# A recurrence with a mixture of experts, first quad: TensorE turns keys, values and results; orders of block beginnings, routed beginning and last stores changed

## The reference

```python
def step(carry, kv_t):                      # over the 128 tokens of a sequence
    p, q, o = carry
    kt, vt = kv_t
    no = jnp.maximum(o, u + kt)
    A = jnp.exp(o - no)
    E = jnp.exp(u + kt - no)
    y = (A * p + E * vt) / (A * q + E)
    no2 = jnp.maximum(w + o, kt)
    A2 = jnp.exp(w + o - no2)
    E2 = jnp.exp(kt - no2)
    return ((A2 * p + E2 * vt, A2 * q + E2, no2), y)

# xf = layernorm(x) as rows
gates = softmax(xf @ gate_w + gate_b)                  # 16 experts
topv, topi = top_k(gates, 2)
combine = sum(one_hot(topi, 16) * topv[..., None], axis=1)
h = gelu(einsum('nd,edh->neh', xf, ew1) + eb1)         # h = 128
eo = einsum('neh,ehd->ned', h, ew2) + eb2
routed = einsum('ned,ne->nd', eo, combine)
hs = gelu(einsum('nd,sdh->snh', xf, sw1) + sb1)        # h = 2048, s = 2
shared = einsum('snh,shd->nd', hs, sw2) + sum(sb2)
x = x + wkv(w, u, layernorm(x), ctx)
x = x + shared + routed
```

## Time and profile before

| | |
|---|---|
| median of 3 runs | 903.01 us (898.25 to 903.58) |
| profiled execution | 902.2 us, its span 900.5 us |
| granted TensorE clock over the span | 0.993 |
| busy of the span | TensorE 93%, VectorE 72%, ScalarE 54%, GpSimd 20% |
| memory traffic | 110.58 MB read, 22.98 MB written |

### The profile page before, as it was taken

One profiled execution on the slowest core, in us unless ns is written; L12 is line 12 of the kernel. 1 busy time (PEld: TensorE's weight loads), 2 busy tenths in 40 slices (PEclk: granted clock), 3 DMA queues, 4 the chain that ended last, 5 costly groups with the idle time before them and its releaser, 6 DMA issues.

```text
span 900.5 us, 14811 instructions
## 1 busy us (share of the span) xinstructions
PE 841.0 (93%) x4018; PEld 694.7 (77%) x4018; DVE 646.8 (72%) x1345; ACT 485.7 (54%) x859; POOL 182.6 (20%) x223
## 2 busy tenths in 40 slices
PE   0198999999999999999999999999999999999997
PEld 0066878888788888887888888878888798997885
DVE  6995899855668687655797777555677588883764
ACT  4433776544455656344556564435455378885531
POOL 2001000011200000111100002111122568763660
PEclk9999999999999999999999999999999999999999
DMA  9155334449543333494343334654797368877985
GB/s 224 28 150 151 111 112 132 114 93 186 108 139 107 99 90 83 101 214 106 118 117 94 94 94 91 127 123 140 176 199 200 106 205 244 258 243 275 305 252 162
DMA packets 125855, 134.40 MB, mean 149 GB/s; under 512 B 10256, under 2 KB 87616, under 8 KB 125276
## 3 DMA queue, kind: packets, MB, share of 16 engines
q1 hardware_dynamic: 116844, 108.47, 46.0%
q0 software_dynamic: 8784, 25.11, 9.5%
q10 hardware_dynamic: 160, 0.02, 0.0%
HBM read 110.58 MB, written 22.98 MB: 148 GB/s over the span
## 4 chain that ended last, share of the span: by engine, by line
PE 92%; DVE 3%; DMA 2%; issue 1%; ACT 1%; SPq 1%; POOL 0%; DVEq 0%; POOLq 0%; ACTq 0%
PE up L561 13%; PE up L562 13%; PE up L563 13%; PE acc L623 12%; PE acc L628 12%; PE acc L625 12%; PE up L770 3%; PE up L772 2%; PE acc L561 2%; PE up L684 1%; PE acc L563 1%; PE acc L562 1%; PE misc L588 1%; PE acc L693 1%; PE up L588 1%
## 5 line engine op out<-in xcount | busy, mean ns | idle before, releaser
L561 PE MATMUL up<-xs,w1hi 128*128 128x512 f32 (+1 forms) x512 | 200.0, 391 | 4.6 <-ACT xs L902 4.6
L562 PE MATMUL up<-xs,w1hi 128*128 128x512 f32 (+1 forms) x512 | 196.5, 384 | 0.0
L563 PE MATMUL up<-xs,w1lo 128*128 128x512 f32 (+1 forms) x512 | 196.4, 384 | 0.0
L623 PE MATMUL acc<-w2hi,hhi 128*128 128x512 f32 x490 | 190.9, 390 | 1.3 <-issue 1.3
L625 PE MATMUL acc<-w2lo,hhi 128*128 128x512 f32 x490 | 190.7, 389 | 0.0
L840 ACT ACTIVATE hhi<-up,b_col 128x512 fp32r<-128x512 f32 (+1 forms) x128 | 86.9, 679 | 148.6 <-PE up L563 119.9
L1058 DVE TENSOR_TENSOR hlo<-hf,hhi 128x512 fp32r<-128x512 f32 (+1 forms) x128 | 86.0, 672 | 88.9 <-ACT hf L843 57.5
L628 PE MATMUL acc<-w2hi,hlo 128*128 128x512 f32 x490 | 131.7, 389 | 0.0
L561 PEld LDWEIGHTS up<-xs,w1hi 128*128 128x128 f32 x512 | 96.2, 188 | 23.9 <-ACT xs L902 5.2
L563 PEld LDWEIGHTS up<-xs,w1lo 128*128 128x128 f32 x512 | 96.2, 188 | 19.2
L562 PEld LDWEIGHTS up<-xs,w1hi 128*128 128x128 f32 x512 | 96.3, 188 | 18.3 <-issue 0.2
(11 more groups left out here) (243 smaller groups left out, 1134.0 us busy)
## 6 DMA issues: line engine op xcount, KB each, us to landing
w_raw<-in_L_ffn_sw SPq DMA_DIRECT2D x270, 256.0 KB, 3.1
expert_rows<-ysb SPq DMA_DIRECT2D x47, 256.0 KB, 3.8
vin<-in_ctx SPq DMA_DIRECT2D x16, 256.0 KB, 8.0
xn_rows<-kn POOLq DMA_DIRECT2D x16, 256.0 KB, 8.4
e2raw<-in_L_ffn_ew SPq DMA_DIRECT2D x16, 256.0 KB, 5.1
ew_sb<-in_L_ffn_ew SPq DMA_DIRECT2D x16, 256.0 KB, 7.5
X<-in_x SPq DMA_DIRECT2D x12, 256.0 KB, 10.1
out<-X SPq DMA_DIRECT2D x12, 256.0 KB, 4.4
```

The costliest lines, as they stand in the source:

```text
L561: nc.tensor.matmul(o, lhs[0], rhs[0], start=start, stop=False)
L562: nc.tensor.matmul(o, lhs[0], rhs[1], start=False, stop=False)
L563: return nc.tensor.matmul(o, lhs[1], rhs[0], start=False, stop=stop)
L623: nc.tensor.matmul(acc[t][:], hh, w2hi[:, slot], start=first and (q > 0 or t >= HT) or again, stop=False)
```

## The change

It has five parts. (1) For the first quad TensorE turns keys, values and results by 128x128 transposes (`key_T`, `value_T`, `result_T`); channels lie in another order than in the other quads, so this quad has small tables and vectors of its own (grow0, boost0, a wider wu), and ScalarE takes the exponential and the copies of values straight from PSUM. The recurrence of this quad is written out in a new order on VectorE (`early_es` and the like), with the product for the next half's keys ahead of the addition of results, which comes from PSUM in two parts. The full tables are made on ScalarE later (the decay's one in the first block), three bias copies go from VectorE to ScalarE, the gate weights go behind the second half's statistics. (2) PRE is 5 instead of 7; SP's first loads are cut by halves, two of the first four loads of x are issued by ScalarE, ahead of w and u, and the weight loads go one for one with the products that free their buffers. (3) At a block's end TensorE runs down product c, then `block_ready` and up product c + 2. (4) At the routed beginning GpSimd's second cast and VectorE's second low part go ahead of the wait for the last shared product, and the third weight and row parts ahead of the X additions; `take_rows` comes one step earlier. (5) Of the last 16 stores SP issues eight and ScalarE eight.

```diff
-    PRE = 7
+    PRE = 5
...
-                    sp.wait_ge(wt.sem, wt.at(2 * q - 1, "tv"))
+                    if q == 1:
+                        sp.wait_ge(vT_ps, TB)
+                    else:
+                        sp.wait_ge(wt.sem, wt.at(2 * q - 3, "tv"))
...
+            load_half(0, (0, 1))
+            load_half(1, range(GB))
+            load_values(0)
+            load_values(1)
...
+            for n in range(RING, PRE + RING):
+                if n < PRE:
+                    load_pre_w1(n)
+                else:
+                    sp.wait_ge(pre_up, n - RING + 1)
+                    load_w1(n - PRE, n - PRE, chunk_of(n - PRE))
+                if n < PRE:
+                    load_pre_w2(n)
+                else:
+                    sp.wait_ge(pre_down, n - RING + 1)
+                    load_w2(n - PRE, n - PRE, chunk_of(n - PRE))
...
+                if c >= RING:
+                    load_w2(c, c, chunk_of(c))
...
-                for g in range(GB):
+                for g in (0, 1):
                     sp.dma_start(outq[NQ - 1, g, :, t], X2[32 * g:32 * g + 32, NQ - 1, t]).then_inc(out_done, 16)
...
-                    if isinstance(c, int) and ahead % CH == 0 and ahead < NCH:
-                        block_ready(ahead // CH)
-                    if not isinstance(c, int) or ahead < HOLD or c >= HOLD and ahead < NCH:
+                    new_block = isinstance(c, int) and ahead % CH == 0 and ahead < NCH
+                    more = not isinstance(c, int) or ahead < HOLD or c >= HOLD and ahead < NCH
+                    if more and not new_block:
                         up_product(c + 2, ahead, ahead // CH)
...
                     last.then_inc(down_done, 1)
+                    if new_block:
+                        block_ready(ahead // CH)
+                        up_product(c + 2, ahead, ahead // CH)
...
+                        pe.wait_ge(con.sem, con.at(0))
+                        pe.wait_ge(bias_hi, 3)
...
+            def key_T(tb):
+                pe.wait_ge(kn_ok, tb + 1)
+                bank = up[tb] if tb < HT else acc[tb - HT]
+                for k in range(KC):
+                    last = nc.tensor.transpose(bank[:, P * k:P * k + P], kn[:, tb, P * k:P * k + P], ident[:])
+                last.then_inc(kT_ps, 1)
...
+            def value_T(tb):
+                pe.wait_ge(v_half[tb // HT], 16 * GB)
+                bank = v_bank[tb]
+                for k in range(KC):
+                    last = nc.tensor.transpose(bank[:, P * k:P * k + P], vin[:, tb, P * k:P * k + P], ident[:])
+                last.then_inc(vT_ps, 1)
+
+            def result_T(tb):
+                pe.wait_ge(wkv0.sem, wkv0.at(tb // HT, "y" if tb % HT else "y0"))
+                bank, at = up[tb] if tb < HT else acc[tb], D * (tb % HT)
+                for k in range(KC):
+                    last = nc.tensor.transpose(bank[:, P * k:P * k + P],
+                                               y_cols[:, at + P * k:at + P * k + P], ident[:])
+                last.then_inc(yT_ps, 1)
...
+            for tb in range(HT):
+                key_T(tb)
+            for tb in range(HT):
+                value_T(tb)
...
+            for tb in range(HT, TB):
+                key_T(tb)
+            value_T(HT)
...
+            value_T(HT + 1)
...
+            for tb in range(HT):
+                result_T(tb)
+            pe.wait_ge(v_ok, TB)
...
+            pe.wait_ge(wexp.sem, wexp.at(1, "e"))
+            pe.wait_ge(ek_half, 2)
...
-                if p == PRE - 2:
+                if p == PRE - 1:
                     for tb in range(HT, TB):
                         transpose_x(tb, xn[:, tb], acc[tb])
                 pre_down_product(p)
+                if p == 1:
+                    for tb in range(HT, TB):
+                        result_T(tb)
...
+            def early_exp(tb):
...
+                nc.scalar.activation(ek[:, :, part], bank[:].rearrange("p (c t) -> p c t", t=TT), ACT.Exp,
+                                     bias=shift[:]).then_inc(wexp.sem if tb % HT else ek_half, 1)
...
+            def early_values(tb):
...
+                nc.scalar.copy((vp1 if tb // HT else vp)[:, :, part],
+                               v_bank[tb][:].rearrange("p (c t) -> p c t", t=TT)).then_inc(v_ok, 1)
...
+            def first_tables():
...
+                for b in range(KC):
+                    last = nc.scalar.activation(grow0[:, b], ramp[:], ACT.Exp, scale=w_down[:, CB + b:CB + b + 1])
...
+            def table_boost():
                 for b in range(CB):
-                    act.wait_ge(tab.sem, tab.at(0))
-                    last = nc.scalar.activation(boost[:, b, TH:], ramp[:, TH:], ACT.Relu, bias=cap_uw[:, b:b + 1],
...
+            def table_keep():
+                act.wait_ge(wkv0.sem, wkv0.at(1))
+                nc.scalar.activation(keep[:, :, 1:], w_neg[:, 0:CB].unsqueeze(2).broadcast_to([P, CB, TH]), ACT.Exp)\
...
+            for g in (2, 3):
+                act.dma_start(X2[32 * g:32 * g + 32, 0, 0:HT], xq[0, g, :, 0:HT]).then_inc(x_half[0], 16)
...
-            tables_first()
-            wkv_exp(0)
-            tables_late()
+            first_tables()
+            for tb in range(HT):
+                early_exp(tb)
+            for tb in range(HT):
+                early_values(tb)
+            table_grow()
+            wkv_reciprocal(0)
             act.wait_ge(b1_ps, 1)
             nc.scalar.copy(b1_col[:], misc[:, 0:CH]).then_inc(b1_ok, 1)
-            act.wait_ge(b1_ok, 1)
-            wkv_reciprocal(0)
-            wkv_exp(1)
+            for tb in range(HT, TB):
+                early_exp(tb)
+            for tb in range(HT, TB):
+                early_values(tb)
+            table_boost()
+            act.wait_ge(c_in, 16 * 10)
+            for part in (0, 32, 64):
+                nc.scalar.copy(bias_r[part:part + 32], bias_f[part:part + 32]).then_inc(bias_hi, 1)
             for tb in range(HT):
                 x_full(tb)
             for tb in range(HT):
                 x_hi_again(tb)
-            for p in range(4):
-                pre_gelu(p)
+            pre_gelu(0)
+            pre_gelu(1)
             nc.scalar.preload_act_table_set("natural_log_exp_and_others")
             wkv_reciprocal(1)
+            pre_gelu(2)
+            pre_gelu(3)
+            split_w1(0, 0)
             pre_gelu(4)
-            split_w1(0, 0)
-            pre_gelu(5)
             split_w1(1, 1)
-            pre_gelu(6)
             for tb in range(HT, TB):
                 x_hi(tb, 1, tb, acc[tb])
             split_w1(2, 2)
...
+                        if r == 2:
+                            table_keep()
...
+            for t in range(TB):
+                act.wait_ge(acc_free, TB * (NQ - 1) + len(y_bank) + t + 1)
+                for g in (2, 3):
+                    act.dma_start(outq[NQ - 1, g, :, t], X2[32 * g:32 * g + 32, NQ - 1, t]).then_inc(out_done, 16)
...
+            def early_es(h):
+                after(wexp, h, "e")
+                dve.wait_ge(ek_half, h + 1)
+                after(tabs0, 0, "grow")
+                if h:
+                    after(wkv0, h - 1, "ev")
+                edo(V.tensor_tensor(by_group(es[:, :, 1:]), by_group(ek[:]), early_times(grow0, h), ALU.mult))
...
+            def early_add(h):
+                for tb in range(HT * h, HT * h + HT):
+                    dve.wait_ge(yT_ps, tb + 1)
+                    bank = up[tb] if tb < HT else acc[tb]
+                    V.tensor_tensor(X2[:, 0, tb], X2[:, 0, tb], bank[:], ALU.add).then_inc(x2_ok, 1)
...
             tables()
             early_ln1(0)
+            early_ln1_apply(0)
             early_ln1(1)
-            early_ln1_apply(0)
-            for part in (0, 2, 3, 4, 5):
-                wkv_part(0, 0, part)
+            early_es(0)
+            early_h(0)
+            early_hv(0)
+            early_den(0)
             early_ln1_apply(1)
-            wkv_key_rows(0, 1)
-            wkv_part(0, 0, 7)
-            wkv_part(0, 0, 8)
+            early_num(0)
+            early_result(0)
+            early_es(1)
+            early_add(0)
             early_ln2(0)
-            wkv_value_rows(0, 1)
+            early_h(1)
             early_ln2_apply(0)
-            for part in (2, 3, 4, 5):
...
+            early_hv(1)
+            early_den(1)
+            early_num(1)
+            early_result(1)
             for tb in range(HT):
                 x_lo_again(tb)
-            wkv_part(0, 1, 7)
-            wkv_part(0, 1, 8)
+            early_add(1)
             early_ln2(1)
+            gate_weights()
             split_w1(0, 0)
+            early_ln2_apply(1)
             split_w1(1, 1)
-            early_ln2_apply(1)
             for tb in range(HT, TB):
                 x_lo(tb, 1, tb, acc[tb])
             split_w1(2, 2)
+            bias_low()
...
             routed_x(1)
+            routed_w1(1)
             dve.wait_ge(down_done, HOLD)
-            routed_w1(1)
             routed_sum(0)
```

(7 more changed lines are left out.)

294 lines of the change are left out of this document (179 added, 115 removed).

## The result

The changed kernel takes 888.42 us (median of four runs, 886.83 to 889.47) where the kernel before takes 901.60 (median of four, 898.25 to 903.58): a ratio of 0.985, with a 95% interval of 0.983 to 0.987; the medians are 13.2 apart. The forecast was 887, within 882 to 893.5. The profiled execution took 888.09, its span is 886.5, 14.0 less than before; the sum of the prediction was 15.05 less.

What follows compares the result with a forecast made beforehand. VectorE's beginning was taken to set when TensorE, nearly gapless after 76.75 us, starts the main products. Terms -14.0 + 5.2 - 4.7 + 0 - 1.85 + 0.3 = -15.05 took 902.2 to 887.2; predicted 887, range 882 to 893.5.

Steps and rivals of the forecast that it cites:

- First half, walked through the list: First quad's start on VectorE: first half's rows at 35.9, so TensorE gets them 6.0 us before today's 41.91.
- the wait for the vectors: Start, loads of small vectors now last of six issues on ScalarE: 4.4 us becomes 6.1, layernorm starts at 7.3.
- one product that hides GpSimd's root: End of VectorE's first half: after statistics at 34.1, a product covers GpSimd's root, rows ready at 35.9.
- The second half: Second half of the first quad: rows at 57.6, then a weight load's cast decides; main products at 62.75, 14.0 earlier.
- rival at 890.0: Two ScalarE table loads on the start's path each add a 1.38 us drain, start 2.8 later; 2%.
- Two chunks less ahead: First block: five chunks in plain f32 instead of seven turn two half steps into full ones, +5.2 us.
- Block beginnings: Down product moved ahead of each block's first up product removes three waits and slow first products: -4.7 us.
- the down product is not ready: Block beginnings keep their wait because the down product moved ahead is not ready: 891.9 us; 6%.
- Routed beginning: Second routed product starts 1.1 us earlier, but VectorE's bank-freeing adds come later: 0, between -1.5 and +1.
- Last stores: End of the kernel: half of the 16 stores issued by ScalarE, last issue at 896.5 instead of 898.4: -1.85 us.
- Row additions: Last chunks: first row additions one step earlier, ahead of a step's low parts, may hold TensorE: +0.3 us, at most 1.
- rival at 903.4: TensorE's short bursts keep it at 1.2 GHz through all plain-f32 products, start at 79, slower than before; 4%.

Runs made afterwards that it cites:

- vectors first: Changed kernel with the four loads of vectors w and u ahead of the two loads of x in ScalarE's queue: 890.73 us.
- tokens-first run: Changed kernel with ScalarE's copies and VectorE's low parts of the second half's tokens ahead of the second chunk's weight split: 885.41 us.
- additions first: Changed kernel with VectorE's two bank-freeing additions put back ahead of the third weight and row parts: 888.81 us.
- filled-gap run: Changed kernel with second half's tokens ahead of the weight split and 74 extra identity turns (28 and 46) in TensorE's idle time: 884.88 us.
- 12 and 16 turns: Changed kernel with 28 extra identity turns on TensorE, 12 ahead of the first half's results and 16 behind them: 889.69 us.

## Why the prediction was right, step by step

- **First half, walked through the list.** TensorE has its rows at 37.37, forecast 35.9: 1.5 late, by two steps that failed. One is the wait for the vectors: forecast 6.1 and statistics at 7.3, measured 6.91 and 8.15, in later traces 7.2 to 7.6. The order of six issues was priced, their landing was not. With the vectors first x is next, at 7.7, so neither order reached 7.3. The other is "one product that hides GpSimd's root": the product took 1.23 as forecast, the root 1.60, and VectorE waited 0.58. It takes 1.60 or 1.61 in all nine traces with the changed start and 0.69 at this place in all five with the old one; why was not tested. Between the two steps the list holds within 0.3, and ScalarE's ramps at 128 columns took 6.24, forecast 6.2.
- **The second half.** VectorE's wait of 2 us for the reciprocal (1.86) and what each engine waits for are right, the times about 1.1 late (result by 51.9, measured 53.0). The cast's load as what ends last: right, shown by the tokens-first run. That the start is only 0.7 late, 63.47 against 62.75, is in part luck: of the 1.5 us, 0.4 came back because the first 24 products took 6.91 instead of 7.33, and the load, issued at 57.61 instead of 56.4, landed after 3.13 us, where I had taken 3.9.
- **The table loads** (rival at 890.0, from the Trainium skill, "ScalarE: Activation LUTs", "What ACT_TABLE_LOAD costs"): the logarithm began 0.02 us after the load's row also here. Had a drain come on top, the path would have shown it. No run shows one.
- **Two chunks less ahead.** 5.24 from the earlier trace rows, and 4.8 measured, on the kernel before (175.9 against 171.1) and on the changed one (174.92 against 170.15 with seven). The first block is 5.5 longer than in the run with only the blocks reordered, because the wait at VectorE's scans is 0.75 longer too (1.85 against 1.10), which I had between -1.1 and +1.1. So the block's total is right by errors that cancel. That it costs nothing ahead holds only in the new beginning; both runs with the other number of chunks are slower.
- **Block beginnings.** -4.7; -1.66 at each of the two later ones in the changed kernel, -5.3 for all three alone, a little more than the waits themselves. The rival "the down product is not ready" has nothing.
- **Routed beginning.** 0, bounds -1.5 and +1: +0.5 over the whole routed part in the changed kernel's trace, 7.45 against 7.38 up to the first down product, and -1.0 there when it ran alone, without a gain in its time. The mechanism was right (VectorE's additions hold the fourth tile's turns), and "what follows these is ready then and starts as today" is nearly so: the third up product comes 5.65 us after the first with the old order, 5.35 with the new one at full clock, and 4.45 with the additions moved back. What I left out is the granted clock. It fell at this beginning in all four traces with the old order, in five of the seven with the wait of 2.5 us, and in none of the three with the additions first.
- **Last stores.** -1.85; -1.8. **Row additions:** +0.3; 0.
- **The low clock.** The granted clock was 0.50 in the first 5 us of a stretch I named as a sign of being wrong (38 to 60), and before it: a window of the changed kernel, same columns as above:

```profile
30.00:42.00 12.00, 5.89 (x21) 4.78 (x22) 11.28 (x17) 8.46 (x15) 2.77 (x3) 0.50 0.22 65
```

It was back at 1.00 by 44, and the chunk products ran at 1.88, so the rival at 903.4 stays out. But the slow phase was in my sum without my seeing it as a cost: I had taken 1.94 and 7.33 from the earlier trace rows, where TensorE had idled 27 us. The filled-gap run prices it: its turns and first products took 2.3 us less than the changed kernel's, 3.2 less than with the tokens first alone, and its start came 3.0 earlier than there.

The errors, 0.7 at the start, next to nothing over the three blocks (+0.53 against +0.5), 0.5 in the routed part and 0.05 at the stores, less 0.3 for the row additions, make the 1.0 by which the forecast gain was too large. The sum is nearer than its terms.

## What to carry to other kernels

Walk the new list of the engine that sets the start, instruction by instruction, with durations from the trace, and let every hand-over end with what it waits for: the end of such a walk came out within 0.8 us of 63, though single steps in it were off by 0.4 to 0.9 us both ways: a load's landing and an operation taken as hidden behind another are the ones to give a range. A cast that waits for a load must not stand ahead of work that is ready and is waited for: moving one such split on each of two engines took away a wait of 1.9 us, and with the additions first the median fell by 4.8. How many products to put ahead of a wait is set by the length of the wait; when the wait changes, count again.

## What the runs showed of the hardware that I had not expected

- A granted clock of 1.00 in a window can mean that the trace has no record there. With the tokens first the first 24 plain products took 7.81 us, with the gap filled 5.45; the windows of 38 to 46, same columns, first of tokens first, then of the gap filled, both say 1.00:

```profile
38.00:46.00 8.00, 7.33 (x23) 5.87 (x24) 7.90 (x8) 3.94 (x6) 1.17 (x2) 1.00 0.23 80
```

```profile
38.00:46.00 8.00, 7.29 (x34) 5.70 (x33) 7.90 (x8) 6.65 (x9) 1.04 (x2) 1.00 0.29 98
```

  But the clock records of the tokens-first trace begin only at 45.30, with the upper level (2.4 GHz), and its products start 0.43 us apart up to 45.33 and 0.22 apart from there on: the lower level (1.2 GHz) before it, unrecorded and shown as 1.00. Where records exist, the spacing changes with them: in the changed kernel at 42.99 and 43.07, in the kernel before at 48.37 and 48.45. In every trace these 24 products took 6.87 us or more where TensorE had idled 3.9 to 27 us ahead of the rows' turns, and 5.45 where it had idled 0.7 or not at all. At a trace's start read the pace from the spacing; the mean clock over a span counts a stretch without records as full speed. The Trainium skill, "TensorE: Matmul & The Clock Gate", "Seeing it yourself", warns that the clock's events have been observed to be unreliable; here the first 45.30 us have no record, while the records that are there agree with the spacing in the two traces just named.
- After a wait of about 2 us the clock falls in some traces and not in others: at the main start in two of four with the wait (vectors first, 12 and 16 turns: 0.56 to 0.62 from 64 to 66, first block 1.6 longer), not in the changed kernel nor with the additions first. Over the nine traces with the changed start there are 20 waits of 1.8 to 2.6 us from the main start on, and at 9 of them the clock fell; where one such fall can be priced, it cost 1.6 us. So a wait can cost more than its length.
- In the last chunks weight loads, gathers and reloaded rows fill the memory queues (DMA share 1.0); there the weights took up to 20.4 us to land (vectors first), and that stretch was up to 0.6, 2.3 or 4.5 us longer; the 4.5 are a wait of 2.6 and a fall of the clock behind it. Two of the nine traces with the changed start show more than 0.6, none of the five with the old one; why is open, and the row additions' place was not shown to matter.
